# First step of a fused norm, convolution and attention kernel written out stage by stage, with later loads issued from ScalarE's DMA queue

## What is computed

```python
x = x + conv_block(ln_c(x), ...)       # ln_c: layer norm over the 256 channels
t = to_tokens(x); t = t + table_ffn(ln_t(t)); x = from_tokens(t)

def conv_block(x, gn_gamma, gn_beta, qkv_w, qkv_b, proj_w, proj_b):
    qkv = conv1d_same(group_norm(x, gn_gamma, gn_beta), qkv_w, qkv_b)   # 256 -> 768 channels, 16 taps
    q, k, v = split(qkv)                                                # 4 heads of 64 channels
    w = softmax(einsum('bct,bcs->bts', q * ch**-0.25, k * ch**-0.25))
    h = einsum('bts,bcs->bct', w, v)
    return x + conv1d_same(h, proj_w, proj_b)                           # 5 taps
```

## Time and profile before

| | us |
|---|---|
| median of 3 runs | 1192.69 (1190.08 to 1196.02) |
| the profiled execution's own time | 1190.26 |
| its span in the trace | 1188.5 |
| PE busy | 1016.5 (86%) |
| DVE busy | 862.2 (73%) |
| ACT busy | 575.1 (48%) |
| POOL busy | 231.3 (19%) |
| mean granted TensorE clock | 0.942 of full |

### The profile page before, as it was taken

How to read it: one execution, slowest core, us unless ns; L and a number is a source line. 1 busy time by engine, 2 the same in 40 slices (tenths; PEclk the granted TensorE clock), 3 DMA queues, 4 the chain that set the end, 5 groups by cost and what they waited for, 6 DMA issues and landing times.

```text
span 1188.5 us, 17778 instructions
## 1 busy us (share of the span) xinstructions
PE 1016.5 (86%) x6760; PEld 670.0 (56%) x6760; DVE 862.2 (73%) x1655; ACT 575.1 (48%) x794; POOL 231.3 (19%) x164
## 2 busy tenths in 40 slices
PE   2737395999999999997989899999999998988854
PEld 1425262666566655664655466656666666756644
DVE  7985976767576578786868566667658675988867
ACT  3443343545445445645547355544435455555522
POOL 2541724100000113112121100000010003223221
PEclk9859697999999999998989899999999999999987
DMA  4240105375275435651654157426533763434412
GB/s 147 80 180 25 45 28 214 74 159 93 50 164 112 80 71 127 145 85 36 195 120 77 36 122 146 89 54 156 95 71 72 191 127 87 107 60 100 107 54 71
DMA packets 279775, 120.44 MB, mean 101 GB/s; under 512 B 267665, under 2 KB 270097, under 8 KB 276753
## 3 DMA queue, kind: packets, MB, share of 16 engines
q1 hardware_dynamic: 279696, 119.37, 43.5%
HBM read 37.43 MB, written 14.81 MB: 44 GB/s over the span
## 4 chain that ended last, share of the span: by engine, by line
PE 45%; DVE 31%; issue 9%; DMA 6%; ACT 5%; POOL 3%; SPq 1%; DVEq 0%; ACTq 0%; POOLq 0%
PE cP L838 11%; PE cM L838 10%; PE cQ L838 8%; PE psV L905 8%; DVE arena L1218 4%; DVE smx L1228 4%; DMA arena<-arena 3%; PE psS L865 3%; PE psT L865 3%; DMA H<-w_qkv 2%; DVE W L1012 2%; DVE W L1005 2%; POOL wsum L466 2%; ACT arena L709 1%; DVE arena L1026 1%
## 5 line engine op out<-in xcount | busy, mean ns | idle before, releaser
L838 PE MATMUL cM<-U,W 128*128 128x256 f16 (+1 forms) x1536 | 230.3, 307 | 47.8 <-ACT m_sb L693 17.8
L838 PE MATMUL cP<-U,W 128*128 128x256 f16 (+1 forms) x1536 | 227.5, 305 | 17.0 <-DVE yqk L1066 11.9
L709 ACT ACTIVATE arena<-arena,smx 128x1024 f16<-128x1024 f32 x128 | 146.8, 1147 | 173.2 <-DVE smx L1261 170.9
L838 PE MATMUL cQ<-U,W 128*128 128x256 f16 (+1 forms) x1536 | 220.6, 300 | 0.0
L838 PEld LDWEIGHTS cM<-U,W 128*128 128x128 f16 x1536 | 152.4, 99 | 120.4 <-ACT m_sb L693 18.1
L838 PEld LDWEIGHTS cP<-U,W 128*128 128x128 f16 x1536 | 151.6, 99 | 84.9 <-DVE yqk L1066 12.2
L838 PEld LDWEIGHTS cQ<-U,W 128*128 128x128 f16 x1536 | 149.2, 97 | 65.1 <-issue 1.6
L1218 DVE SCALAR_TENSOR_TENSOR arena<-arena,smx 128x1024 f16<-128x1024 f32 x128 | 167.6, 1309 | 20.0 <-ACT arena L709 19.9
L905 PE MATMUL psV<-arena 128*128 128x512 f16 x512 | 124.0, 398 | 37.4 <-DMA arena<-arena 37.4
L1270 DVE SCALAR_TENSOR_TENSOR arena<-psV,arena 64x512 f32<-64x512 f32 x32 | 22.0, 689 | 152.0 <-ACT arena L716 151.9
L687 ACT ACTIVATE arena<-psS,smx,esc 128x1024 f32<-128x1024 f32 x64 | 76.9, 1202 | 75.1 <-DVE smx L1229 75.1
(11 more groups left out here) (196 smaller groups left out, 1235.6 us busy)
## 6 DMA issues: line engine op xcount, KB each, us to landing
U<-kept_u SPq DMA_DIRECT2D x6, 2077.0 KB, 9.9
H<-w_qkv SPq DMA_DIRECT2D x12, 1024.0 KB, 7.6
kept_u<-U SPq DMA_DIRECT2D x2, 2077.0 KB, 10.3
kept_u<-arena SPq DMA_DIRECT2D x2, 2077.0 KB, 6.9
arena<-x_tok SPq DMA_DIRECT2D x8, 512.0 KB, 9.0
W<-x_tok SPq DMA_DIRECT2D x4, 1024.0 KB, 6.1
out_tok<-W SPq DMA_DIRECT2D x3, 1024.0 KB, 4.3
kept_h<-arena SPq DMA_DIRECT2D x4, 514.0 KB, 4.5
```

The costliest lines, as they stand in the source:

```text
L709: a(phl[:, i % 3, 0, :], prob[:, i % 2, :], ACT.Copy, scale=smx[:, i % 2, 4:5]) \
L838: last = mm(out, W[:, j, wl, c, wat + tap, :], U[:, slot, ul, c, at:at + width], start=(c == 0 and tap == 0 and wl + ul == 0), stop=(c == ...
```

## The change

1. **Step 0 written out.** Every engine gets a list by hand, `first_step`, in which the pieces of the input side and of the weights stand one by one among the convolution's. `wst` becomes two buffers: tile 1 loads into a second one (`wst_b`) at once, and loads come in quarters of 512 KB. Only the layer norm, transposes and group norm of all four batches, and U of batches 0 and 1, stay in step 0. The batches come in the order 0, 1, 3, 2 (`BATCH_AT`); eo of batch 3 is stored (`keep_eo`) and loaded again.
2. **U of batches 2 and 3** is made in steps 1 and 2 (`batch_split`: slots 3, 5, 7), right into the slot of U that the next step reads. `load_u` is only left for steps 4 to 7. `diff` of batch 1 goes from POOL to DVE.
3. **Weight scale.** The two maxima on DVE become two sums of squares on ACT (`squares`, Square with accumulated output), the power of two comes from half the exponent (`squared=True`).
4. **Two small operations per unit**, the scaled negative maximum and the scaled reciprocal, go from DVE to ACT.
5. **The copies of k** go from DVE to a DMA on SP's queue (`copy_k`, 64 partitions by 4 KB, two per step).
6. **ACT's DMA queue.** `load_u` in four quarters and `load_w` of tiles 3, 4, 5 in four quarters each are issued by ACT. SP keeps the transposes, the stores, `copy_k` and the loads of the start and the end.
7. **Places.** Weight pieces in steps 3 and 4 are spread over more slots; the reading of `psV` (`heads`) comes a slot later on ACT and DVE; the spread of y's maximum (`y_top`) comes at a slot's end. The loops of steps 1, 2, 5, 6 are written out.

```diff
-        aside = arena[:, edge[-1] - CT * UW:edge[-1]].bitcast(F16).rearrange("p (l c w) -> p l c w", l=2, c=CT)
+        WST = CT * 2 * PH_TAPS * P
+        wst_b = arena[:, edge[-1] - WST:edge[-1]].rearrange("p (c s k o) -> p c s k o", c=CT, s=2, k=PH_TAPS)
+        BATCH_AT = (0, 1, 3, 2)
...
         def u_home(b):
-            return (U[:, 1], U[:, 0], aside, aside)[b]
+            return U[:, (b + 1) % 2]
...
         EXTRA = {
-            0: table(batch_input(1, 0, 4, 4, 7, 7, 7, 10), tile_weights(1, (1, 1, 2, 2, 2, 2, 2, 2, 2, 2, 2)),
-                     batch_input(2, 6, 10, 10, 13, 13, 13, 14), tile_weights(2, (8, 8, 9, 9, 9, 9, 9, 9, 9, 9, 9)),
-                     batch_input(3, 13, 16, 15, 17, 17, 17, 17), [(4, ("wtop", 1)), (10, ("wtop", 2)), (17, ("ring", 0))]),
-            3: table(tile_weights(3, (1, 3, 4, 4, 5, 6, 8, 8, 9, 10, 10)), tile_weights(4, (12, 14, 15, 15, 16, 17, 17)),
+            1: table(batch_split(2, 3, 5, 7), [(1, ("ring", 0))]),
+            2: table(batch_split(3, 3, 5, 7)),
+            3: table(tile_weights(3, 0, 1, 2, 2, 3, 4, 5, 5, 6, 6, 7, 8),
+                     tile_weights(4, 13, 14, 15, 15, 15, 16, 16, 17, 17)),
...
             def load_w(m):
-                if m >= 1:
-                    sp.wait_ge(S["wlo_done"], PARTS * m)
+                if m == 2:
+                    sp.wait_ge(S["wlo_done"], PARTS)
...
+            def copy_k(k, hd):
+                sp.wait_ge(S["qk_lo"], 2 * (2 * k + hd + 1))
+                sp.dma_start(stack[0:D, hd, 1:3, :].rearrange("p k t -> p (k t)"),
+                             stack[D:P, hd, 1:3, :].rearrange("p k t -> p (k t)")).then_inc(S["qk_done"], 16)
...
-            sp.wait_ge(S["u_out3"], 16)
+            keep_eo()
+            copy_k(0, 0)
             for k in range(STEPS):
                 for u in range(UNITS):
                     turn(k, u)
-                    if u == 4 and k < STEPS - 2:
-                        load_u(k + 2)
+                    if u == 4:
+                        copy_k(k, 1)
+                    if u == 14 and k < STEPS - 1:
+                        copy_k(k + 1, 0)
...
+            def squares(m, c):
...
+                a(junk, wst(m)[:, c].rearrange("p s k o -> p (s k) o"), ACT.Square,
+                  accum_out=am[:, 4 + c:5 + c]).then_inc(S["c_m"], 1)
...
+            def load_u(n, q):
+                act.wait_ge(S[f"u_out{n % NB}"], 16)
+                act.wait_ge(S["conv_done"], GROUPS * TILES * (n - 1) + 1)
+                act.dma_start(Uf[(n + 1) % 2][:, q * UN // 4:(q + 1) * UN // 4], kept_u[n % NB][:, q * UN // 4:(q + 1) * UN // 4]) \
+                    .then_inc(S["u_in"], 16)
...
+                        act.wait_ge(S["mx_done"], 16 * k + u + 1)
+                        a(smx[:, u % 2, 1:2], smx[:, u % 2, 0:1], ACT.Copy, scale=esc[:, hd, 1:2]).then_inc(S["nb_done"], 1)
...
+                    if conv and NB <= n + 1 < STEPS and 4 <= i < 8:
+                        load_u(n + 1, i - 4)
+                    if n == 2 and 12 <= i < 16:
+                        load_w(3, i - 12)
...
-                    ch.wait()
-                    ch.step(v.tensor_copy(stack[0:D, hd, 1, :], stack[D:P, hd, 1, :]))
-                    v.tensor_copy(stack[0:D, hd, 2, :], stack[D:P, hd, 2, :]).then_inc(S["qk_done"], 1)
...
+            def first_step():
...
+                layer_stats(1)
+                weights("wadd", 1)
+                weights("wscale", 1)
+                layer_norm(1)
+                weights("wsum0", 1)
+                half_y(0, 0, 0, 0)
+                finish_y(0, 0, 0)
+                layer_stats(2)
+                weights("wsum1", 1)
+                scale_y(0, 0, 0)
+                layer_norm(2)
```

More of the change, by code:

```diff
@@ L670, in step @@
+            def step(n, p, attn, conv):
                 k = n - 1
                 for i in range(SLOTS if conv else LAST):
-                    for entry in EXTRA.get(more, {}).get(i, []):
-                        extra(*entry)
+                    unit = attn and i < UNITS
                     if attn and i == 0:
@@ L1275, in step @@
+                    if attn and i in (6, 10, 14):
+                        heads(k, i // 4 - 1)
+                    if not conv and i == 17:
+                        heads(k, 3)
+                    for entry in EXTRA.get(n, {}).get(i, []):
+                        extra(*entry)
                     if not conv:
@@ L1308 @@
+            first_step()
+            for n in range(1, STEPS):
+                step(n, n // NB, True, True)
+            step(STEPS, PAIRS, True, False)
 def kernel(x, L0_conv_gn_gamma, L0_conv_gn_beta, L0_conv_qkv_w, L0_conv_qkv_b, L0_conv_proj_w, L0_conv_proj_b):
```

850 lines of the change are left out of this document (523 added, 327 removed).

## The result

| | before | after |
|---|---|---|
| median, us | 1192.7 (1190.1 to 1196.0, 3 of 4 runs) | 1221.0 (1219.0 to 1224.8, 4 runs) |
| span of the profiled execution | 1188.5 | 1222.6 |
| PE / DVE / ACT busy, us | 1016.5 / 862.2 / 575.1 | 1034.4 / 763.4 / 653.9 |
| mean granted TensorE clock | 0.942 | 0.936 |

The ratio after to before is **1.0239, 95% interval 1.0193 to 1.0285**: slower, by 28 us and 114 us above the forecast; whether by 2% the interval leaves open. DVE is busy 99 us less, and the time went up all the same. The kernel before has a fourth time in this comparison, 3784.5. Why it stands so far out no run shows; it would lift the median to 1194.4, and it has no part in the ratio.

A forecast was written before the change was run, and what follows sets the result against it. PE was taken to bound plain steps and DVE's list step 0. Gains of 37 + 9 + 15 + 12 + 4 + 8 = 85 us from the profiled 1190.3 gave 1105, written as 1107 for a median; range 1080 to 1140.

The forecast's parts named there:

- minus 15 and minus 12: Steps 3 and 4: earlier weight maximum and spread pieces end PE's waits, giving 113 and 112 us; together minus 12 to 33.
- minus 1 per plain step: Four plain steps: last unit done some 3 us earlier, less the copy of k ahead of its transpose; minus 8 to plus 8.
- Forecast end 150: Step 0: bound by DVE's list of 113 us from 26 us, plus 11 of waits; ends at 150, minus 37.
- the four places of 3 to 4 us: Step 0: waits found by following the five engines' lists; 11 us was taken for them.
- The rival with 172: Rival 2, step 0: one wait turns into another, 33 us of waits stay, the whole at 1129 us; chance 0.19.
- the term of minus 9: Step 1: two PE waits of 13.4 us go and 2 to 4 us remain; minus 9, between minus 4 and minus 13.
- The floor of 109: Steps 3 and 4: the plain step's length, 109 us, taken as the least they could reach.
- Rival 1: Steps 3 and 4: loads interleave, transposes as late as before; 11 of 27 us gain lost, 1118 us; chance 0.14.
- my criterion: Plain steps: over 111 us would prove the forecast wrong, with the tiny operations on ACT or the copies costing time.
- Rival 4: Every head: DMA copy of k exposed beyond 4.7 us of cover, each microsecond costing 16; slower; chance 0.03.
- minus 8: Last stage: two copies of k and 5.8 us of small operations leave DVE; minus 8, between 0 and minus 15.
- My 0.95 for faster: Whole kernel: chance 0.95 of being faster by more than about 0.5%, 6 us; within 0.01, slower 0.04.

The follow-up runs named there:

- the other four places undone: Changed kernel with loads on SP, scale chain and heads in their old slots, and copy of k behind the last transpose: 1172.2 us, ratio 0.982.
- kernel of 1145 us: Changed kernel, five places undone: loads on SP, old scale and heads slots, copy of k last, weight pieces early in their slots: 1145.0 us, ratio 0.960.

## Why the prediction was wrong, point by point

In short: what the change takes from DVE was forecast well (step 0 and below). The step that failed is that edits of order were given no price, or a gain. "Pieces are spread over more slots" counted as gain alone in the minus 15 and minus 12 of steps 3 and 4, the net of minus 1 per plain step priced the copy's delay but not what waits behind it, and a second queue was worth "no gain" at worst. The runs put 76 us on five such places.

**Step 0: right.** Forecast end 150, measured 150.4, in every run between 150 and 153.4. The two terms were each off and made up for each other: DVE's list was put at 113 and is 105.1, so it idled 19 us and not 11 (the four places of 3 to 4 us that I had counted make 12 to 16 already). PE has one wait of 7.4 us, where none above 5 was named. That the end came out to the microsecond is luck. The rival with 172 is out.

**Step 1: the term of minus 9 was plus 4.** Where 114 was forecast, 126 came. The scale chain, heads and the copy's place, each undone alone, give 3 to 4 of it, all five places together 5. In the 120.9 that remain, against 109.2 for step 2 before, PE waits 3.9 us for the first copy of k behind the stores of U and eo and 6.3 us for transposes, at a clock of 0.96. I had given these 2 to 4 us in all. And the 13.4 us to be saved were counted wrong: the wait of 6.5 us ends at 187.22, the mark, so it lies in step 0, whose end I had moved already, and only the 6.9 were step 1's. The transposes of v wait 7.9 us in the same place now, ahead of 150.8. With 6.9 the term would have been minus 3 to minus 5.

**Steps 3 and 4: minus 15 and minus 12 became plus 12 and plus 28.** The step that failed is "pieces are spread over more slots", which I took as gain alone. The change also moved them to a slot's end, and I gave that no price; with the other four places undone it cost 10 and 16 us (137 to 127, 136 to 120). The queue cost 12 and 15 us as the last of the five. In step 3 these overlap, since all five undone give back 12 there, and 34 in step 4. DVE's work fell as forecast, to 86.3 us in step 3, and the waits for the weight maximum did fall, from 5.0 and 5.8 to 1.9 and 0.2, so that half of the mechanism was right. The floor of 109 was not reached even at best. ACT is busy 84 and DVE 87 of 127 us in step 3, and the units' chain goes back and forth between them; that this is the reason is argued, no run tests it.

**The queue.** Rival 1 named the right mechanism and the wrong size and sign. I priced a second queue as "no gain", 11 us; it is a loss of 5 us on the changed kernel and 24 on the better one, each with the moments of issue that go with the queue. The Trainium skill (DMA: Bandwidth & Descriptors, section "Issuing engines are not separate DMA queues") says that DMAs of different issuers interleave on the same sixteen engines; the landing of 20.4 us beside a median of 4.3 agrees that they share. The same page (section "Queues, rings and completion order") says that an engine takes turns between its queues packet by packet. No run shows single turns, and by this rule alone the halved GB/s would not follow.

**Every step: minus 1 became plus 5, and plus 10 in step 2.** DVE is busy 63.6 us in a plain step, the forecast's 64. I wrote that the copy of k stands ahead of the last transpose "which costs 1.3 plus an issue", and set 3 us of gain from the earlier reciprocal against it. The delay was right (1.9 us at 907.08 to 908.98). What I left out was its consequence: it ends in PE's wait, behind which the product runs at a granted clock of 0.69 (5.03 for 3.61 us). And the gain of 3 us was eaten by `heads` in slot 14, which I did not price either. In step 2 `heads` back alone takes 119.4 to 111.8, so the split added there costs little, as forecast. With the copy last, heads and scale back, the plain step is 107.8, at the forecast's 108 to 109. Of my criterion "over 111, then the tiny operations on ACT or the copies cost" the copies' place was it, together with `heads`, which the criterion did not name; the tiny operations were not.

**Rival 4, an exposed copy of k.** Its landing is 3.8 us in the median, inside the 4.7 of cover. It is exposed once, 3.9 us in step 1. The loss came through the queue behind it, a path that the rival did not have.

**The last stage: minus 8 became plus 1.5.** DVE's list fell from 148.9 to 135.5 us as forecast. PE waits 6.0 us for the late scale chain and 13.8 for transposes. With all five places undone it is 179.5, minus 6.5, within the 0 to 15 given.

**The sum.** 1221 against 1107 is 114. Five undone places are 76 of it. The other 38 are terms that were too hopeful. Against the lengths before less each term, the kernel of 1145 us is longer by 14.5 us in step 3, 8 in step 1, 6 in step 4, 3 each in steps 2 and 7, 2 in step 0 and the last stage together, and shorter by 1.5 in steps 5 and 6, 35 in all; of the 8 in step 1, 6.5 are the wait counted twice. Some 3 are the difference between profiled and median runs. (The forecast wrote 112 for step 4 from a length of 123 to 125; between the transposes of v it is 125.7.) Of these 35 us no run undoes a cause. My 0.95 for faster rested on sizing only the listed edits of work; the edits of order were counted at nothing.

## What to carry to other kernels

Price every instruction that changes its place, not only those that appear or go: name what stands behind it in its queue, and ask what each of its waits holds up. In a chain of small units a piece with a wait on two other engines belongs where its wait is covered, not in front of the next unit. Here large loads did best in the queue of the latency-bound transfers; measure a second queue before believing in it, and when several orders change at once, undo them one at a time and then together: alone the queue cost 5 us and the pieces' place 11, as the last of several 24 and 27.

## What the runs showed of the hardware

- Transposes and loads on one queue: busy share 1.05 to 1.08, 207 to 247 GB/s, landing in 7.4 us at most in step 3. The same loads from a second queue, issued some us earlier: busy share 1.17 to 1.39, 86 to 105 GB/s, landing in up to 20.4 us. A packet of a transpose took 88 ns there and 21 ns alone. With the second issuer the engines moved half as much.
- It did so only in bursts: two plain steps with four quarters of U from ACT beside transposes from SP lost 0.5 and 0.7 us.
- A wait named "issue" in the row of a matmul group was a semaphore of a DVE chain whose last operation had ended 0.10 us before.
- 32 operations of 0.2 to 0.3 us per step on ACT instead of DVE cost nothing that can be told: the move back gives plus 3 us, with intervals of the ratios that overlap. The squares on ACT in place of the maxima were not tried alone.
